# An attention and feed-forward layer: the shift moved ahead of the value matmuls, and own heads first on VectorE

## What is computed

```
content  = einsum('bhqd,bhkd->bhqk', q, k)
relative = einsum('bhqd,qkd->bhqk', q, rel_k[idx])
w = softmax((content + relative) / sqrt(8))
out = einsum('bhqk,bhkd->bhqd', w, v) + einsum('bhqk,qkd->bhqd', w, rel_v[idx])
x + (out @ Wo.T + bo) + ffn(layernorm(x))
```

## Time and profile before

| | |
|---|---|
| median of 3 runs | 470.05 us (469.66 to 472.0) |
| the profiled execution | 470.23 us |
| its span in the trace | 468.4 us |
| mean granted TensorE clock | 0.983 of full speed |
| busy, share of the span | PE 89%, DVE 87%, ACT 89%, POOL 67% |

### The profile page before, as it was taken

The page is one execution under the profiler, slowest core; times in us unless marked ns, Lnnn a source line. Parts: engine busy times, 40 slices in busy tenths (PEclk is TensorE's granted clock), DMA queues, the critical chain, the costliest instruction groups (busy, mean ns, idle before and its releaser), DMA issues.

```text
span 468.4 us, 24907 instructions
## 1 busy us (share of the span) xinstructions
PE 418.0 (89%) x10258; PEld 337.8 (72%) x10258; DVE 407.1 (87%) x887; ACT 416.4 (89%) x806; POOL 314.1 (67%) x370
## 2 busy tenths in 40 slices
PE   0888888689999999999999999999999999999863
PEld 0345554477888888888888888888788888788753
DVE  8879766549999999999999999999999999999875
ACT  2889999459999999999999999999999999999810
POOL 6557777616675767687776868786778777686520
PEclk9999999889999999999999999999999999999987
DMA  7624745963112525424252524242543515244786
GB/s 160 216 65 121 128 90 133 164 134 79 27 37 57 75 59 85 83 68 78 61 94 47 86 48 83 60 71 62 93 76 64 96 36 94 50 85 92 152 184 186
DMA packets 159529, 43.09 MB, mean 92 GB/s; under 512 B 122321, under 2 KB 156601, under 8 KB 159289
## 3 DMA queue, kind: packets, MB, share of 16 engines
q1 hardware_dynamic: 152304, 40.19, 41.9%
q10 hardware_dynamic: 7112, 1.31, 1.8%
HBM read 21.55 MB, written 16.79 MB: 82 GB/s over the span
## 4 chain that ended last, share of the span: by engine, by line
PE 52%; issue 12%; ACT 9%; DVE 6%; POOL 0%; ACTq 0%; DVEq 0%; POOLq 0%
PE ps_s L1031 10%; PE ps_s L1026 10%; PE ps_s L1133 10%; PE ps_o L1048 9%; PE ps_t L1118 7%; DVE mx L1243 5%; PE ps_r L1072 5%; ACT xr L1169 4%; ACT big L1204 4%; PE ps_s L1108 1%; ACT p L1184 1%; PE ps_r L252 1%; DVE big L1247 1%; POOL big L872 0%; ACT ps_y L1184 0%
## 5 line engine op out<-in xcount | busy, mean ns | idle before, releaser
L872 POOL TENSOR_TENSOR big<-p,big 128x512 f16<-128x512 f32 x128 | 148.6, 1161 | 102.8 <-ACT big L1204 102.1
L1031 PE MATMUL ps_s<-by_q_room,e 96*128 96x64 f16 x2048 | 103.2, 192 | 0.0
L1026 PE MATMUL ps_s<-qbd,kst 96*128 96x128 f16 x1024 | 99.5, 219 | 2.9 <-PEq L300 2.5
L1247 DVE TENSOR_TENSOR big<-ps_y,big 128x512 f16<-128x512 f32 x128 | 88.1, 688 | 15.6 <-ACT big L1204 13.9
L1287 DVE TENSOR_REDUCE mcol<-ps_t 128x4 bf16<-128x512 bf16 x128 | 87.6, 684 | 9.9 <-PE ps_t L1118 5.9
L1243 DVE TENSOR_TENSOR mx<-s,ps_s 128x512 bf16<-128x512 bf16 x128 | 86.7, 677 | 3.2 <-ACT s L1162 2.1
L1162 ACT ACTIVATE s<-ps_s 128x512 bf16<-128x512 f32 x128 | 80.3, 627 | 5.9 <-PE ps_s L1031 5.9
L1031 PEld LDWEIGHTS ps_s<-by_q_room,e 96*128 96x128 f16 x2048 | 85.4, 97 | 0.1
L1204 ACT ACTIVATE big<-p 128x512 f16<-128x512 f32 x128 | 84.7, 662 | 0.0
L1184 ACT ACTIVATE ps_y<-ps_s 128x512 f32<-128x512 f32 x128 | 76.0, 594 | 8.7 <-PE ps_s L1133 4.7
L276 POOL COPY by_q_room<-qrel 96x256 uint32<-96x256 uint32 x128 | 78.5, 630 | 3.4 <-POOLq L300 3.1
(11 more groups left out here) (110 smaller groups left out, 530.8 us busy)
## 6 DMA issues: line engine op xcount, KB each, us to landing
rel_dram<-xr SPq DMA_DIRECT2D x32, 256.0 KB, 3.3
xr<-rel_dram SPq DMA_DIRECT2D x60, 128.0 KB, 3.6
kst<-big SPq DMA_DIRECT2D x48, 64.0 KB, 2.0
qrel<-qr_dram SPq DMA_DIRECT2D x192, 16.0 KB
qbd<-q_dram SPq DMA_DIRECT2D x192, 16.0 KB
y_dram<-big SPq DMA_DIRECT2D x4, 512.0 KB, 2.9
big<-y_dram SPq DMA_DIRECT2D x4, 512.0 KB, 5.8
out<-big SPq DMA_DIRECT2D x8, 256.0 KB, 3.2
```

Source lines behind the costliest of these rows:

```text
L872: nc.gpsimd.tensor_tensor(probs[:, k // 8, 1, 1, k % 8, :], p32[:, k % 2, 1, :], probs[:, k // 8, 0, 1, k % 8, :], ALU.subtract).then_inc( ...
L1026: nc.tensor.matmul(bank[:, P * g:P * g + P], kst[:, g, S * k + P * kh:S * k + P * kh + P], rhs, start=(g == 0), stop=False, skip_group_che ...
L1031: ins = nc.tensor.matmul(bank.rearrange("p (h q j) -> p h q j", q=Q0, j=J)[:, :, q, :], e4[:, first:first + P], rhs.rearrange("p (h j) -> ...
L1247: nc.vector.tensor_tensor(probs[:, k // 8, 1, 0, k % 8, :], ps_y[:, :], probs[:, k // 8, 0, 0, k % 8, :], ALU.subtract).then_inc(lo0_ready, 1)
```

## The change

Two moves in the loop, one on each of two engines. On TensorE the shift of unit n comes directly behind the scores of unit n+1, and the value matmuls follow it, for unit n-2 instead of n-3, directly ahead of the relative ones. So the last step also does the value matmuls of the last unit but two, and those behind the loop are dropped. On VectorE own heads of unit n-3 comes ahead of the low part and the maximum; the sum over heads stays last. Nothing is added or removed in all.

```diff
@@ -1124,9 +1124,6 @@
                     if qb == 0 and k == 0:
                         down_part(nc, v, ps_r[:, :], range(FT), None)
                         add_bias(nc, v, ps_r[:, :], 0).then_inc(rest_ready, 1)
-                    if unit(qb, k - 3):
-                        pv(*unit(qb, k - 3))
-
                     pe.wait_ge(mcol_ready, n + 1)
                     for kh in range(KH):
                         for g in range(G):
@@ -1134,12 +1131,13 @@
                                                    mcol[:, k % 2, g:g + 1].to_broadcast([P, P]), negid[:, :],
                                                    start=False, stop=(g == G - 1), skip_group_check=True)
                         ins.then_inc((shifted0, shifted)[kh], 1)
+                    if unit(qb, k - 2):
+                        pv(*unit(qb, k - 2))
                     relative_step(qb, k)
 
             pe.wait_ge(v["kst_in"], 16 * PARTS * G * (NCH // 2 - 1))
             scores(0, 0)
             loop(pe, body)
-            pv(NQB - 1, UNITS - 3)
             project(0)
             pv(NQB - 1, UNITS - 2)
             for part in range(4):
@@ -1293,14 +1291,14 @@
                                                 v["x_sb"][:, own, :], ALU.add).then_inc(rest_added, 1)
                         dve.wait_ge(rest_added, 1)
                         nc.vector.memset(ps_r[:, :], 0.0).then_inc(rel_zero, 1)
+                    if unit(qb, k - 3):
+                        own_heads(*unit(qb, k - 3))
                     if unit(qb, k - 1):
                         low_part(*unit(qb, k - 1))
                     if k < UNITS - 1:
                         maximum(qb, k + 1)
                     elif not last:
                         maximum(qb + 1, 0)
-                    if unit(qb, k - 3):
-                        own_heads(*unit(qb, k - 3))
                     for piece in range(4):
                         m = block_at(qb, k, 25 + piece)
                         if m is not None:
```

## The result

| | before | changed |
|---|---|---|
| median | 470.61 us (7 runs) | 466.90 us (7 runs, 465.04 to 467.83) |
| ratio, 95% interval | | 0.9915 (0.9895 to 0.9936) |
| span of the profiled execution | 468.4 us | 465.1 us |
| 104 steps of the loop (16 to 119) | 281.54 us | 279.63 us |

What follows compares the result with a forecast made beforehand. Before, TensorE bounds fast steps and the exponential's late start the slow ones; after, VectorE's loop bounds fast steps. Gains of 4.3 us in cycles and 0.7 at the edges make 470.1 - 5.0 = 465 us, range 460.5 to 472.

Steps and rivals of the forecast that it cites:

- The bound of the fast step: VectorE's loop from transposes to next transposes (T to T) bounds steps without ScalarE's move: mean 2.58 us, before 2.60.
- The spacing of 0.20: On VectorE, the low part starts 0.20 us after own heads starts; at 0.25 the cycle is even with before.
- rival B: Own heads costs 0.32 ahead of VectorE's low part: fast steps 2.70, 475 us; chance 0.10, softer form 0.05.
- The slow step: Every fourth step, with ScalarE's move: 2.89 us instead of 2.98, exponential 2.03 after the transposes start (T), not 2.14.
- C: Slow step doesn't shorten: exponential still starts at T + 2.14, only fast steps gain, 468.3 us; chance 0.18.
- TensorE's need: TensorE's time in a fast step falls from 2.60 to 2.42 us, two tiling changes fewer at about 0.09 each.
- D: Adjacent value and relative matmuls still pay 0.09 on TensorE: it needs 2.51, time as forecast; no chance of its own.
- rival A: TensorE was the whole bound: fast steps 2.42, cycle 10.2 by ScalarE's 21 ops at 0.485, 454 us; chance 0.07.
- Value matmuls one unit younger: On TensorE, they need POOL's low part by T + 1.75; it ends at T + 1.44 at the latest, covered by 0.3.
- The sum: Four-step cycle 3 x 2.58 + 2.89 = 10.63 against 10.78: 0.16 gained in 26.75 cycles, 4.3 us; with edges 5.0.
- scattered disturbance: Remainder from the loop's 10.78 us cycle to the observed 10.83, some 1.2 us over 26 cycles before the change.
- The edges at the end: Last group's TensorE-bound steps gain 0.4 us in all, the tail's last exponential comes 0.1 earlier; all edges together 0.7.

Runs made afterwards that it cites:

- the doubled own heads: Changed kernel with own heads masked twice on VectorE, the first time into a tile nobody reads: 484.88 us, ratio 1.0295 against the kernel before.
- The run without eight matmuls: Changed kernel without the eight value matmuls a step that take the low part of the values: 462.84 us, ratio 0.9809 against the kernel before.
- two halves of this one: Changed kernel with own heads back behind the maximum: 554.65 us; kernel before with own heads ahead of the low part: 550.97 us.
- a third split: Kernel before with only the shift moved ahead of the value matmuls, which keep unit n-3; own heads stays: 466.23 us, ratio 0.9892.

## Why the prediction was right, and where it was off

- **The bound of the fast step** (VectorE's loop, 2.58): right. It is 2.57, with a reciprocal 2.59; the doubled own heads show that each 0.20 there comes out in full. This holds for this order: with the shift alone a step without reciprocal is 2.49, bound by ScalarE.
- **The spacing of 0.20** from own heads to the low part, the number between gain and loss: measured 0.20. The Trainium skill (VectorE: DVE Perf Modes, The DRAIN you can't avoid) says that the next op doesn't start until the pipe is empty, and adds in the same paragraph that an op which isn't held starts earlier. The trace agrees with the addition, which rival B left out: the low part starts 0.08 ahead of own heads' recorded end.
- **The slow step** (2.89): right, 2.88 or 2.89, so C is out. The exponential starts at T + 2.02 (forecast 2.03), 0.78 after the start of the low part that reads `ps_y` (forecast 0.79). The sign that the trace would name the low part as its releaser didn't come in the changed kernel; it is named 53 times with own heads doubled.
- **The shift** at T + 1.2: 1.19. **TensorE's need** of 2.42: 268.04 less 265.62 is 2.42. Its busy share: 93%, as said. That adjacent value and relative matmuls pay no gap is shown by 0.34 for 24 matmuls, so D is out too; the Trainium skill's rule (TensorEngine Tiling (Array Packing), Key Properties) fits, and rival A, which built on it, is out because TensorE was not the only bound.
- **Value matmuls one unit younger** cost nothing: the waits list none for POOL.
- **The sum.** The cycle was to gain 0.16 and gained 0.16 (10.79 to 10.63, by the medians of the steps). What was off is the "scattered disturbance" of 1.2 us, which I carried over unchanged without asking what it was. Part of it were only the steps of 2.62; above the medians the stretch lies 0.9 us before, and 3.2 and 1.2 in the two traces of the changed kernel. So the 104 steps, forecast to gain 26 x 0.16 = 4.2, gained 1.9 in one trace and 4.0 in the other. The edges at the end were off too: from step 120 to the end it took 47.8 before and 48.2 and 48.4 after, where I had 0.5 less; 0.7 and 1.1 us of stalls lie there. The run without eight matmuls shows what both are: without stalls the 104 steps take 276.60, and the end 47.1. 5.0 forecast, 4.0 measured.
- **Luck.** The traces hold one microsecond that isn't the change's. Step 0 is 6.38 us before and 5.39 and 5.37 after; over all traces of both orders it is either 5.33 to 5.62 or 6.38 to 6.77. From step 1 to the end the two traces gained 2.0 and 4.0 us: how near an execution comes to the forecast also hangs on how many stalls it happens to have.
- **Rival A's floor** of ScalarE, 21 ops at 0.485 = 10.2, was too low. Where ScalarE has no idle time it takes 3 x 2.49 + 2.98 = 10.45. It changed no chance here, but it did mislead my expectation for the shift alone.
- **What the prediction didn't ask** is which of its moves pays. The shift alone takes 466.23 us, the whole change 466.90.

## What to carry to other kernels

Price a moved op by the spacing of starts, not by its duration, and ask on whose ring of waits it lands: here the same 0.20 us was free behind the maximum and cost 0.20 a step ahead of it. Split a change before you credit its parts, and into every part that can stand alone: two halves of this one cost 80 us each, which makes all of it look needed, and a third split gave the whole gain by itself. Don't carry small disturbances over into a forecast before looking into a few of them; gaps inside a group of equal instructions have no semaphore to blame, and their places in the program, taken modulo 256, can show what they have in common. And in a loop with 150 or more TensorE instructions in 2.6 us, count instructions as well as time.

## What the runs showed of the hardware that I had not expected

TensorE can run short of instructions. In the changed kernel, at 152 matmuls and weight loads a step of 2.66 us, the stalls are 2 to 4 us in all, with 24 more a step 24 to 31 us, even where the added matmuls have only 2 columns, and with 16 fewer none. In the order before they are 0.3 us, and 10 with 24 more. Steps of 3.34 and 3.36 us (each part alone) had none. All 161 stalls stand at the same place of a block of 256 instructions (number 193 or 194). The eight longest of the changed kernel end 2.2 to 2.9 us after the start of a 16 KB packet of the instruction queue, whose own transfer takes about 1.1 us. When such a packet is asked for, and why the order before stalls less, stays open.
